# Experts of an attention and feed-forward block: Silu on ScalarE for tanh and a VectorE product, and a weight-spreading product of 128 rows

## The reference

```
x = x + grouped_attention(layernorm(x), ctx, ctx)
x = x + routed_experts(layernorm(x))
x = x + latent_attention(layernorm(x), ctx)
x = x + quantised_ffn(layernorm(x))
```

```
probs = softmax(x @ classifier.T);  idx = top_k(probs + bias, 2)
w = 1.5 * probs at idx, else 0
out = sum over experts e: w[e] * ((silu(x @ gate[e].T) * (x @ up[e].T)) @ down[e].T)
    + x * sum(w of the identity routes)
```

## Time and profile before

| | us |
|---|---|
| median of 3 runs | 924.28 (923.9 to 924.57) |
| the profiled execution, its own time | 926.4 |
| its span | 924.8 |
| TensorE busy, over the span | 811.0 (88%) |
| VectorE / ScalarE / GpSimd busy | 667.6 / 395.6 / 502.7 |
| rows are turned, with route logits | 177.0 to 190.8 |
| the routes and 32 expert steps | 191.0 to 389 |
| rows are turned again | 390.9 to 402.4 |
| latent attention | to 757 |

### The profile page before, as it was taken

How to read it: one execution, slowest core, us unless ns; L and a number is a source line. 1 busy time by engine, 2 the same in 40 slices (tenths; PEclk the granted TensorE clock), 3 DMA queues, 4 the chain that set the end, 5 groups by cost and what they waited for, 6 DMA issues and landing times. The chain is left out here.

```text
span 924.8 us, 15048 instructions
## 1 busy us (share of the span) xinstructions
PE 811.0 (88%) x4785; PEld 568.8 (61%) x4792; DVE 667.6 (72%) x1203; ACT 395.6 (43%) x1056; POOL 502.7 (54%) x495
## 2 busy tenths in 40 slices
PE   3999999679989898579999999999999979766775
PEld 2554544347767677456777777776777659653443
DVE  4898987468887878647666666666666725998894
ACT  2687877322222222123444444444444363213442
POOL 3555555216665656505555555555555549535774
PEclk9999999779999999959999999999999979888999
DMA  9100000040000000030101101010000000000001
GB/s 270 59 1 0 0 1 1 0 151 18 18 17 18 17 17 0 9 117 12 46 1 46 38 11 46 0 45 0 1 1 1 1 1 2 0 0 1 29 29 35
DMA packets 8755, 24.54 MB, mean 27 GB/s; under 512 B 1711, under 2 KB 4143, under 8 KB 8087
## 3 DMA queue, kind: packets, MB, share of 16 engines
q1 hardware_dynamic: 8154, 23.81, 7.7%
q10 hardware_dynamic: 549, 0.08, 0.1%
HBM read 21.79 MB, written 2.10 MB: 26 GB/s over the span
## 5 line engine op out<-in xcount | busy, mean ns | idle before, releaser
L1122 PE MATMUL ps<-yt_all,a 128*128 128x512 f32 x576 | 140.9, 398 | 0.0
L1284 POOL TENSOR_TENSOR p<-p,l_inverse 128x512 f32<-128x512 f32 x64 | 66.5, 1039 | 125.9 <-DVE l_inverse L1247 125.9
L1122 PEld LDWEIGHTS ps<-yt_all,a 128*128 128x128 f32 x576 | 106.4, 189 | 26.2 <-issue 5.0
L773 PE MATMUL ps<-yt_experts,wsplit 128*128 (+1 forms) x384 | 102.5, 419 | 10.0 <-DVE h L867 8.3
L1202 ACT ACTIVATE p<-ps,l_negmax 128x128 f32<-128x128 f32 x256 | 89.8, 377 | 37.3 <-DVE l_negmax L1254 37.3
L1254 DVE TENSOR_REDUCE l_negmax<-ps 128x4 f32<-128x512 f32 x64 | 41.3, 687 | 81.9 <-PE ps L1165 81.9
L1233 DVE TENSOR_TENSOR turned<-ps,rope 128x1024 f32<-128x1024 f32 x64 | 78.3, 1224 | 29.3 <-PE ps L1122 25.5
L394 DVE TENSOR_REDUCE negmax<-ps 128x4 f32<-128x512 f32 x128 | 85.4, 688 | 11.5 <-PE ps L243 9.6
L773 PEld LDWEIGHTS ps<-yt_experts,wsplit 128*128 128x128 f32 x384 | 75.0, 202 | 28.3 <-DVE inner L861 7.6
L1142 PE MATMUL ps<-q,b 128*128 128x512 f32 x192 | 88.5, 597 | 1.0 <-issue 1.0
L325 ACT ACTIVATE pt<-ps 128x512 f32<-128x512 f32 x128 | 72.8, 596 | 8.3 <-PE ps L263 4.1
(11 more groups left out here) (185 smaller groups left out, 1662.3 us busy)
## 6 DMA issues: line engine op xcount, KB each, us to landing
wide<-in_wide SPq DMA_DIRECT2D x8, 768.0 KB, 4.2
mx_raw<-in_mx SPq DMA_DIRECT2D x8, 384.0 KB, 3.1
x<-in_x SPq DMA_DIRECT2D x4, 512.0 KB, 8.7
ctx_t<-in_ctx_t SPq DMA_DIRECT2D x1, 2048.0 KB, 7.8
narrow<-in_narrow SPq DMA_DIRECT2D x8, 256.0 KB, 4.5
out<-x SPq DMA_DIRECT2D x16, 128.0 KB, 1.7
ktraw<-in_ctx_rows SPq DMA_DIRECT2D x1, 1248.0 KB
wraw<-in_gate SPq DMA_DIRECT2D x1, 1024.0 KB, 18.2
```

Of the source, the lines that this page charges most:

```text
L773: t = pe.matmul(out, w_at(pw, w + k * EXPERTS * INTER + x * INTER, INTER), run_of(m.yt[:, py, k, :, :], j).rearrange("p b s -> p (b s)"), ...
L1122: t = pe.matmul(tile_ps[k], a[par][:, pa, kin, k * 128:(k + 1) * 128], m.yt[:, py, kin, 4 * j:4 * j + 4, :].rearrange("p b s -> p (b s)"), ...
L1284: pool.tensor_tensor(p[:, head, :, :], p[:, head, :, :], spread(inverse[:, head, :], 2, S), ALU.mult).then_inc(normed[head], 1)
```

## The change

- VectorE's `gated` is gone. ScalarE computes Silu(gate) into `gated` instead of tanh into `tanh`, and VectorE's `inner` is a plain product of `gated` and up. The waits move with it: ScalarE may write a buffer of `gated` when `inner` of two units before is made.
- The tables `weights` and `select` have 128 rows in place of 40; the new rows hold zeros. The transposes L759 turn 128 columns, the ScalarE copy L814 takes 128 rows, the subtraction L848 32 rows in place of 8, and L780 multiplies 128 rows.
- The memset of `weights` (2048 columns now, 640 before) and the making of `select` leave the start of `routed_experts` and become GpSimd's program in the first `turn_rows`. Their semaphores last for the whole program.

The diff:

```diff
--- before.py
+++ after.py
@@ -39,6 +39,7 @@
 
 
 EXPERTS, ZERO, INTER = 8, 4, 128
+LO, WROWS = 32, 128
 ROUTES = EXPERTS + ZERO
 TOP_SCALE = 1.5
 ROUTE_STEPS, ROTARY_STEPS = 21, 5
@@ -600,6 +601,13 @@
                 logits(GROUPS - 2)
                 logits(GROUPS - 1)
 
+        @block.gpsimd
+        def _(pool):
+            if routes:
+                pool.memset(m.r_weights[:, :, :], 0.0).then_inc(m.w_zero, 1)
+                pool.tensor_tensor(m.r_select[:, :, :], spread(m.ident[:, 0:EXPERTS], 2, 128),
+                                   spread(m.ident[:, LO:LO + EXPERTS], 2, 128), ALU.add).then_inc(m.selected, 1)
+
         @block.scalar
         def _(act):
             def keep_logits(j):
@@ -679,14 +687,10 @@
         sem = lambda name: scope.enter_context(nc.semaphore(name))
         N = 4 * S
         UNITS = GROUPS * EXPERTS
-        LO = 32
-        WROWS = LO + EXPERTS
         r = RouteTables(sb)
         factor, offset = sb("r_factor", [S, B, 1]), sb("r_offset", [S, B, 1])
-        weights = sb("r_weights", [S, B, WROWS])
+        weights, select = m.r_weights, m.r_select
         weights_t = sb("r_weights_t", [WROWS, GROUPS, N], F32R)
-        select = sb("r_select", [WROWS, EXPERTS, 128], F32R)
-        tanh = [sb(f"tanh{i}", [INTER, N]) for i in range(2)]
         gated = [sb(f"gated{i}", [INTER, N]) for i in range(2)]
         inner = [sb(f"inner{i}", [INTER, N]) for i in range(2)]
         h = [sb(f"h{i}", [INTER, N]) for i in range(2)]
@@ -703,10 +707,9 @@
         w_at = lambda part, c, width: m.wsplit[:, part, c:c + width]
 
         logits_turned, route, centred, exp_made = sem("logits_turned"), sem("route"), sem("centred"), sem("route_exp")
-        selected, affine, affine_made = sem("selected"), sem("affine"), sem("affine_made")
-        w_zero, w_turned, w_hi, w_lo = (sem(n) for n in ("w_zero", "w_turned", "w_hi2", "w_lo2"))
-        gate_made, up_made, tanh_made, gated_made, inner_made = (
-            sem(n) for n in ("e_gate", "e_up", "e_tanh", "e_gated", "e_inner"))
+        affine, affine_made = sem("affine"), sem("affine_made")
+        w_turned, w_hi, w_lo = (sem(n) for n in ("w_turned", "w_hi2", "w_lo2"))
+        gate_made, up_made, gated_made, inner_made = (sem(n) for n in ("e_gate", "e_up", "e_gated", "e_inner"))
         weight_spread, h_made, h_hi, h_lo, down_made = (sem(n) for n in ("e_weight", "e_h", "e_h_hi", "e_h_lo", "e_down"))
         x_made, parts_made, stats_made, var_made = (sem(n) for n in ("e_x", "e_parts", "e_stats", "e_var"))
         rotated = sem("rotated")
@@ -760,7 +763,7 @@
                                          m.ident[:, :])
                     t.then_inc(w_turned, 1)
                 pe.wait_ge(w_lo, GROUPS)
-                pe.wait_ge(selected, 1)
+                pe.wait_ge(m.selected, 1)
 
             def step(u, j, x):
                 par, old = x % 2, 1 - x % 2
@@ -817,8 +820,8 @@
                 par, old = x % 2, 1 - x % 2
                 if inside(u, UNITS):
                     act.wait_ge(gate_made, u + 1)
-                    wait(act, gated_made, u - 1)
-                    act.activation(tanh[par][:, :], gate_ps[par], ACT.Tanh, scale=0.5).then_inc(tanh_made, 1)
+                    wait(act, inner_made, u - 1)
+                    act.activation(gated[par][:, :], gate_ps[par], ACT.Silu).then_inc(gated_made, 1)
                 if inside(u - 1, UNITS):
                     act.wait_ge(h_made, u)
                     wait(act, down_made, u - 2)
@@ -845,21 +848,16 @@
             def routes():
                 for g in range(GROUPS):
                     dve.wait_ge(w_hi, g + 1)
-                    dve.tensor_tensor(weights_t[LO:, g, :], m.bank(6 + g % 2)[LO:WROWS, :],
-                                      weights_t[LO:, g, :].bitcast(F32), ALU.subtract).then_inc(w_lo, 1)
+                    dve.tensor_tensor(weights_t[LO:2 * LO, g, :], m.bank(6 + g % 2)[LO:2 * LO, :],
+                                      weights_t[LO:2 * LO, g, :].bitcast(F32), ALU.subtract).then_inc(w_lo, 1)
 
             def step(u, j, x):
                 par, old = x % 2, 1 - x % 2
                 if inside(u, UNITS):
-                    dve.wait_ge(tanh_made, u + 1)
-                    wait(dve, inner_made, u - 1)
-                    dve.scalar_tensor_tensor(out=gated[par][:, :], in0=tanh[par][:, :], scalar=1.0, in1=gate_ps[par],
-                                             op0=ALU.add, op1=ALU.mult).then_inc(gated_made, 1)
                     dve.wait_ge(gated_made, u + 1)
                     dve.wait_ge(up_made, u + 1)
                     wait(dve, h_made, u - 1)
-                    dve.scalar_tensor_tensor(out=inner[par][:, :], in0=gated[par][:, :], scalar=0.5, in1=up_ps[par],
-                                             op0=ALU.mult, op1=ALU.mult).then_inc(inner_made, 1)
+                    dve.tensor_tensor(inner[par][:, :], gated[par][:, :], up_ps[par], ALU.mult).then_inc(inner_made, 1)
                 if inside(u - 1, UNITS):
                     dve.wait_ge(weight_spread, u)
                     dve.wait_ge(inner_made, u)
@@ -922,7 +920,7 @@
             dve.tensor_tensor(r.biased[:, :, :], logit_ps, spread(r.total[:, :], 2, ROUTES), ALU.subtract).then_inc(centred, 1)
             dve.wait_ge(exp_made, 1)
             choose_routes(dve, m, r, then)
-            dve.wait_ge(w_zero, 1)
+            dve.wait_ge(m.w_zero, 1)
             for rows in (0, LO):
                 then(dve.tensor_copy(weights[:, :, rows:rows + EXPERTS], r.e[:, :, 0:EXPERTS]))
             then(dve.tensor_reduce(r.total[:, :], r.e[:, :, EXPERTS:], AX.X, ALU.add))
@@ -932,10 +930,6 @@
 
         @block.gpsimd
         def _(pool):
-            pool.memset(weights[:, :, :], 0.0).then_inc(w_zero, 1)
-            pool.tensor_tensor(select[:, :, :], spread(m.ident[0:WROWS, 0:EXPERTS], 2, 128),
-                               spread(m.ident[0:WROWS, LO:WROWS], 2, 128), ALU.add).then_inc(selected, 1)
-
             pool.wait_ge(route, ROUTE_STEPS)
             pool.tensor_tensor(factor[:, :, 0], r.total[:, :], m.rstd[:, :, 0], ALU.mult).then_inc(affine, 1)
             pool.wait_ge(affine, 1)
@@ -1666,6 +1660,7 @@
         self.rope, self.kvr = sb("rope", [128, 6, S]), sb("kvr", [S, B, CE])
         self.keys = sb("keys", [2 * CE, B, S])
         self.stored = scope.enter_context(nc.semaphore("stored"))
+        self.w_zero, self.selected = sem("w_zero"), sem("selected")
         self.rope_loaded = scope.enter_context(nc.semaphore("rope_loaded"))
         self.pause, self.pool_pause, self.eps = sb("pause", [S, 1]), sb("pool_pause", [S, 3]), sb("eps", [S, 1])
         self.ident16 = sb("ident16", [128, 128], BF16)
@@ -1693,6 +1688,8 @@
                 grouped_attention(nc, m)
             m.logits_t = experts.enter_context(nc.sbuf_tensor("logits_t", [ROUTES, GROUPS, 4 * S], F32))
             m.yt = experts.enter_context(nc.sbuf_tensor("yt_experts", [128, 2, HALVES, B, S], F32R))
+            m.r_weights = experts.enter_context(nc.sbuf_tensor("r_weights", [S, B, WROWS], F32))
+            m.r_select = experts.enter_context(nc.sbuf_tensor("r_select", [WROWS, EXPERTS, 128], F32R))
             turn_rows(nc, m, routes=True)
             with ExitStack() as context:
                 m.ctx_t = context.enter_context(nc.sbuf_tensor("ctx_t", [2 * CE, 2, B, S], F32))
```

## The result

The changed kernel takes **916.2 us** (median of 4 runs, 911.3 to 917.4) beside 924.4 for the kernel before on the same chip: ratio 0.9898, 95% interval 0.9858 to 0.9938. It is 8 us faster, inside the range of the prediction and only half of the 17 us that it gave.

What follows compares the result with a forecast made beforehand. TensorE was taken to set the pace in the 32 expert steps. Terms of -13.1 (22 steps), -3.4 (six before) and -0.4 (the one before those) made -16.9, from 924.3 to 907.4 us; range 902 to 917.

Steps and rivals of the forecast that it cites:

- rival A: Expert groups' seventh steps: the clock falls all the same, or L1300 comes too late; 916.5 us, chance 0.2.
- Height of L780: Expert steps, TensorE: going from 128 rows to 40 and back opens gaps around the weight-spreading product; 0.37 us a step.
- Rival B: Expert steps: the gaps around L780 are not of its height, only the stalls shrink; 912.7 us, chance 0.1.
- Does VectorE let TensorE have it?: Expert steps: VectorE's chain ties with TensorE, 4.52 against 4.50 us; a pair becomes 9.10 us, eleven pairs give -7.9 us.
- gated gone from VectorE: Before a group's seventh step: L1300 gets in ahead of L951, TensorE's stall is 1.5 us instead of 2.07; -0.55 a group.
- The clock behind the stall: Seventh step of each group: TensorE's clock stays at full behind the shorter wait for h; -1.6 us a group.
- x: Third step of each group: TensorE's wait for VectorE's addition to x grows from 1.22 to 1.61 us; +0.4.
- Silu's table loads: ScalarE, ahead of the first Silu and first Exp: two added loads of 1.28 us are hidden; nothing.
- Tables made earlier: Stage that turns rows: GpSimd's memset and select, about 2.0 + 1.9 us, delay nothing; 0.
- rival C: Stage that turns rows: GpSimd's table work blocks VectorE, with TensorE behind it, for 3.9 us; 911.3 us, chance 0.06.

Runs made afterwards that it cites:

- change again: The changed kernel, unaltered, profiled and timed once more beside the kernel before: 915.7 us, ratio 0.9894.
- Silu alone: Kernel before with only ScalarE's Silu replacing tanh and VectorE's product; tables of 40 rows where they were: 914 us, ratio 0.9889.
- Move alone: Kernel before with only its two 40-row table operations moved to where rows are turned; tanh stays: ratio 1.0012.
- 128 rows alone: Kernel before with only the tables raised to 128 rows, made where they were; tanh and VectorE's product stay: 924.1 us, ratio 0.9993.
- tables back: The changed kernel with both 128-row table operations issued at the start of the routed experts again: median 3 us below the change timed beside it.
- factor moved: The changed kernel, table operations back at the experts' start, GpSimd's product of x by its factor at x = 5, not 3: 906.3 us, ratio 0.9819.
- tables late: The changed kernel with GpSimd's table operations still where rows are turned, but waiting until all 16 VectorE normalisations are made: ratio 0.9883.

## Why the prediction was right, and where it was not

The time fell into the range, and faster was right. But the range reached up to 917 us only for rival A (916.5), and A isn't what happened: L1294 came ahead of L945 and the clock stayed. That 916.2 lies inside is in part luck. Term by term:

- *Height of L780*: the gaps are of the height, as argued: 0.39 us and 0.23, both with Silu and without, and 64 rows behave as 40. Rival B is out. The size was a little high: an undisturbed pair went from 9.84 to 9.27 us, 0.28 a step and not 0.37, since the even step gave only 0.22 to 0.30.
- *Does VectorE let TensorE have it?* This step failed. I checked one step's chain (4.52 us against 4.50) and took the pair of 9.10 for every pair. GpSimd and VectorE have work that comes once a group (L945, the statistics, the rotation), and a quicker TensorE runs into it: in change again, from 260.35 to 300.79, it is 1.15 us more in the sixth step, 0.20 in the seventh, 0.16 in the eighth, 0.37 in the first, 1.54 in the third, 3.4 us on top of the 37.1 that a group would take. The height, put at 10.5 us over the 29 steps (7.9 + 3 x 0.72 + 0.4), gave 1.1 on top of Silu.
- *gated gone from VectorE*: the order at L1294 and L945 came as forecast, with 0.13 us to spare where 0.15 had been worked out, but the term was too small. I left a stall of 1.5 us and it is 0.76 with 128 rows and 0.2 with 40. Silu alone gave 13.6 us in place of the 6.4 that the sum held beside the height. Without the clock, that is 10 us in place of 1.6. The two errors made up for each other, and the experts' total looked right: 14.6 against 16.9. That was luck; without the two parts run alone it would have passed as a confirmation.
- *The clock behind the stall*: kept at full, as forecast, but its 3 x 1.6 us were too much and too sure. "Move alone" has before's experts and waits 1.92 us for h at the same three places. Behind the first wait its products take 2.99 us, and the granted clock is 1.00 from 278.90 to 284.30:

```profile
281.74 2.99 PE L778 MATMUL ps<-yt_experts,wsplit 128*128 x12 [1.92 <-DVE h L872]
```

  Its three seventh steps take 5.43, 6.63 and 5.42 us, those of before 6.58, 6.62 and 6.61. So a fall costs 1.2 us, and behind the same wait it comes at one time and not at another. "128 rows alone" waited 2.27 us there and kept its clock all three times. The 2.4 us between 160.5 and 158.2 are two falls. Without falls, before's middle stretch is 157.0 us, by either profile (an estimate: 160.5 - 3 x 1.2, 158.2 - 1.2). Against that the rows alone give 0.1 us, Silu alone 10.1 and both 11.1.
- *x*: expected 0.4 us more a group, measured idle times of 1.70, 1.38 and 1.66 against 0.92, so 0.5 to 0.8 more.
- *Silu's table loads*: nothing, as forecast. Behind its 1.28 us load the first Silu starts 0.01 us later. The 1.38 us of drain that the Trainium skill counts (ScalarE: Activation LUTs, What ACT_TABLE_LOAD costs) isn't in these rows either.
- *Tables made earlier*: put at 0, given 0.06 as rival C, and this is what happened. VectorE's normalisations waited for GpSimd, and the way to the third step took 3.8 us more in the profiles, 1 to 2 by the ratios, where the prediction's price was 3.9. The argument against it read L405's sixteen durations as proof that the form doesn't block. It was none: the stage they are from has GpSimd operations, but only two of the sixteen L405 have one beside them, and the other fourteen say nothing about a conflict that they never met. Neither of the two was held up (0.41 and 0.40 us), but GpSimd's operations beside them had one and four columns, where the memset has 2048. The right rows were L1300 and L1301, the same instruction and held up both times, which the prediction itself named and set aside. The Trainium skill's rule (SBUF — State Buffer, Who interferes with whom) that the loser of the shared port pair blocks fully fits the 1.97 us for a normalisation beside a 1.80 us memset. It doesn't fit the L405 at 17.62 us, which took its 0.40 us inside a GpSimd operation of four columns (16.92 to 18.06); no run here shows why.

The remainder. The profiled execution of before was 2.0 us above its kernel's median and that of after 1.1 below; 11.3 us between the spans less 3.1 is the 8.2 between the medians. The times go with the steps without falls: Silu alone is 10.3 us faster by its ratio and 10.1 by its steps, tables back 11.7 and 11.1, the rows alone 0.6 and 0.1, factor moved 16.7 and 16.3. So the falls in the profile of before seem to be missing in most of its executions. This is inferred: only a profiled execution shows where its clock fell. The sum now: 11.1 from the experts' steps, less 1 to 2 for the turning of rows, leaves 9 to 10, beside the measured 8.2 with its interval of 5.7 to 13.1. By this count the forecast of 16.9 had 4.8 for a clock that mostly didn't fall, and nothing for the turn of rows.

## What to carry to other kernels

Before a gain per step is multiplied by the number of steps, lay out what the other engines must do in a whole period, the work that comes once a period included: the bound is there, and after the bottleneck has been made quicker it is the place to move work from (1.9 us of GpSimd's work moved by two steps gave 5 us). Work that is "moved to where the engine idles" is free only if nobody else is using what it uses; look for a moment at which both do run before you call a row evidence. And when a change has two parts, run each alone, since a right total can be made of two wrong terms.

## What the runs showed that was not expected

- At the start of the stage that turns rows, VectorE got exactly one of its tensor_scalar operations in per GpSimd operation: three normalisations in 5.69 us beside three operations of 1.80, 1.83 and 1.93. A memset, which reads nothing, held it up as the others do.
- The longest stretch at half clock in the stage that turns rows was 17.1 us in each of the four profiles with GpSimd's work beside its start, and 10.2 to 13.7 us in the ten others. The clock came back later where TensorE's work began later. Over the first 15 us the granted clock was 0.57 to 0.61 in the four, and 0.68 to 0.83 in before, "tables back" and "tables late".
- Nearly the same code behind the experts took 551.3 to 557.2 us from one kernel to the next. The longest ones also had the longest sum of half-clock stretches there (557.2 and 556.7 us with 86 us of them, 551.6 and 551.9 us with 62 to 63), but the relation is loose: the shortest, 551.3, had 69, and one of 553.4 had 83. A change of 2 us is below what one profile can show here.
